# Banded attention of a two-layer decoder: output products moved behind the next group's projections, q, k and v projections in three split terms, head weights streamed in parts

## What is computed

```python
q = einsum('bth,oh->bto', x, wq)      # 16 heads of 128
k = einsum('bth,oh->bto', x, wk)      # 4 heads of 128, each shared by 4 query heads
v = einsum('bth,oh->bto', x, wv)
q, k = rope(q), rope(k)
scores = einsum('btgrd,bsgd->bgrts', q, k) / sqrt(128)
scores = where((s <= t) & (t - s <= 128), scores, min)
out = einsum('bgrts,bsgd->btgrd', softmax(scores), v)
return einsum('bto,ho->bth', out, wo)  # added to x
```

## Time and profile before

| | |
|---|---|
| median of 3 runs | 2412.54 us (2406.25 to 2413.64) |
| the profiled execution | 2406.55 us, span 2404.8 us |
| PE busy over the span | 2151.0 us (89%) |
| DVE busy | 1712.6 us (71%) |
| POOL busy | 1048.7 us (44%) |
| ACT busy | 944.7 us (39%) |
| DMA | 214.87 MB, mean 89 GB/s |

### The profile page before, as it was taken

One profiled execution on the slowest core, in us unless ns is written; L12 is line 12 of the kernel. 1 busy time (PEld: TensorE's weight loads), 2 busy tenths in 40 slices (PEclk: granted clock), 3 DMA queues, 4 the chain that ended last, 5 costly groups with the idle time before them and its releaser, 6 DMA issues. The chain is left out here.

```text
span 2404.8 us, 24923 instructions
## 1 busy us (share of the span) xinstructions
PE 2151.0 (89%) x7344; PEld 1108.7 (46%) x7344; DVE 1712.6 (71%) x2983; ACT 944.7 (39%) x1808; POOL 1048.7 (44%) x798
## 2 busy tenths in 40 slices
PE   6998999899999977997889898999789999999858
PEld 2554445454455543443555555465333433334234
DVE  1787788768876885786889889889546364654554
ACT  1443344333333433764655646465123232332311
POOL 2343354333333440322899998999511011010142
PEclk9999999999999998998999999999889999999979
DMA  7000000000000002455644526353332122221121
GB/s 263 19 19 18 19 20 20 18 18 22 22 18 19 23 23 90 159 186 214 266 162 166 197 105 210 127 203 108 107 80 78 41 77 57 70 70 46 52 109 53
DMA packets 95563, 214.87 MB, mean 89 GB/s; under 512 B 15832, under 2 KB 33112, under 8 KB 93032
## 3 DMA queue, kind: packets, MB, share of 16 engines
q1 hardware_dynamic: 77192, 156.18, 19.8%
q10 hardware_dynamic: 17760, 57.42, 6.7%
...
q0 software_dynamic: 512, 0.13, 0.0%
...
## 5 line engine op out<-in xcount | busy, mean ns | idle before, releaser
L759 POOL TENSOR_SCALAR a_prob<-a_prob,a_rsum 128x256 f32<-128x256 f32 x256 | 146.6, 590 | 467.3 <-DVE a_rsum L687 467.1
L1455 POOL TENSOR_TENSOR s_state<-s_b_rows,s_delta_u 128x1024 f32<-128x1024 f32 x128 | 303.5, 2384 | 36.9 <-DMA s_b_rows<-scan_bc 34.4
L1499 DVE TENSOR_TENSOR_SCAN s_state<-s_decay,s_state 128x512 f32<-128x512 f32 x256 | 304.9, 1211 | 15.5 <-ACT s_decay L1441 13.2
L1614 PE MATMUL c_bank<-c_xn_parts,c_w_parts 128*128 128x512 f32 (+1 forms) x1056 | 269.5, 405 | 6.2 <-DMA c_w_parts<-ffn_weights_lo 6.2
L1441 ACT ACTIVATE s_decay<-s_delta,s_a 128x512 f32<-128x512 f32 x256 | 173.5, 689 | 226.1 <-DVE s_state L1499 220.6
L491 PE MATMUL a_bank<-a_xn_t,a_wq 128*128 128x512 f32 x512 | 227.3, 592 | 0.0
L602 ACT ACTIVATE a_prob<-a_score,a_neg_m 128x256 f32<-128x256 f32 x256 | 117.6, 475 | 279.0 <-DVE a_neg_m L682 278.8
L1614 PEld LDWEIGHTS c_bank<-c_xn_parts,c_w_parts 128*128 128x128 f32 (+1 forms) x1056 | 196.3, 187 | 65.8 <-issue 20.3
L574 PE MATMUL a_bank<-a_wo,a_out_t 128*128 128x512 f32 x512 | 222.3, 593 | 0.0
L2049 ACT ACTIVATE d_prob_t<-d_score 128x512 f32<-128x512 f32 x256 | 138.9, 595 | 192.2 <-PE d_score L1931 191.1
L373 DVE TENSOR_SCALAR f_picks<-f_mask,f_lut_xor,f_lut 128x260 int32<-128x260 int32 x512 | 202.3, 468 | 9.6 <-DVE f_mask L367 0.5
...
...
## 6 DMA issues: line engine op xcount, KB each, us to landing
s_b_rows<-scan_bc SPq DMA_DIRECT2D x64, 512.0 KB, 3.7
c_w_parts<-ffn_weights_hi ACTq DMA_DIRECT2D x39, 512.0 KB, 3.6
c_w_parts<-ffn_weights_lo ACTq DMA_DIRECT2D x39, 512.0 KB, 4.5
...
d_qs<-d_hi SPq DMA_DIRECT2D x128, 64.0 KB, 2.0
d_ks<-d_hi SPq DMA_DIRECT2D x128, 64.0 KB, 2.0
d_factor<-in_factors SPq DMA_DIRECT2D x16, 512.0 KB, 3.6
```

Of the source, the lines that this page charges most:

```text
L1455: pool.tensor_tensor(self.state[:, s], row.broadcast_to([P, 2, T]), self.delta_u[:, h % 2], ALU.mult) \
L1499: dve.tensor_tensor_scan(self.state[:, s, e, :], self.decay[u % 2][:], self.state[:, s, e, :], 0.0, ALU.mult, ALU.add).then_inc(self.scann ...
L1614: mm = nc.tensor.matmul(banks[b][0:width[o], :], w_parts[:, n % SLOTS, w, at:at + width[o]], xn_parts[:, x_, k, :], start=((k, w, x_) == t ...
```

## The change

Three things change in the attention stage.

First, the weights of the projections and the normalized features are kept as two f32r parts, a rounded one and the remainder, and a bank of q, k or v is the sum of three products (both rounded parts, and each remainder with the other's rounded part): 12 single instructions for 8. The features are drained by both engines, ACT rounding and DVE subtracting. Head weights no longer stay in SBUF. SP loads each head's raw weights (256 KB), ACT rounds and POOL subtracts, SP stores both parts in DRAM, and later passes load them from there, 512 KB a head, each when the head's bank of the group before is full. `passes` writes the first pass out apart from the loop.

Second, PE computes the output products of group g - 1 in group g, behind its projections and ahead of its turns. In group 0 the values of the same batch row stand there. Group 3 has its own output products at its end too.

Third, the groups take 4, 4, 3 and 5 chunks of the lookup instead of 4 each. DVE's adds stand between the picks and choices of the chunks, the loads of wo and of the batch rows of x are issued by SP and not by ACT, and the second and third rope of a group follow the exponentials of both later heads.

```diff
+    GROUPS = (0, 4, 8, 11, PER_PASS)
...
+class HeadWeights:
...
+    def load_piece(self, sp, m, source):
+        if m >= 2:
+            sp.wait_ge(self.split, m - 1)
+        sp.dma_start(self.raw[:, m % 2, :], source).then_inc(self.raw_in[m % 2], 16)
+    def load_raw(self, sp, n, p):
+        if n:
+            sp.wait_ge(self.stored[p], 16 * n)
+        self.load_piece(sp, self.piece(n, p), self.dram["head_w"][:, n * self.STEPS + p, :])
+    def load_parts(self, sp, g, p, after_stores=None):
+        if after_stores:
+            sp.wait_ge(self.stored[p], 16 * after_stores)
+        sp.dma_start(self.parts[:, p].bitcast(F32), self.scratch["head_parts"][:, g * self.STEPS + p]) \
+            .then_inc(self.ready[p], 16)
+    def store(self, sp, n):
+        for p in range(self.STEPS):
+            sp.wait_ge(self.ready[p], 16 * (n + 1))
+            sp.dma_start(self.scratch["head_parts"][:, n * self.STEPS + p], self.parts[:, p].bitcast(F32)) \
+                .then_inc(self.stored[p], 16)
+    def round_piece(self, act, m, hi):
+        act.wait_ge(self.raw_in[m % 2], 16 * (m // 2 + 1))
+        self.nc.scalar.copy(hi, self.raw[:, m % 2, :]).then_inc(self.rounded, 1)
+    def round(self, act, n, steps):
+        for p in steps:
+            self.round_piece(act, self.piece(n, p), self.parts[:, p, 0, :])
+    def subtract(self, pool, n, steps):
+        for p in steps:
+            m = self.piece(n, p)
+            pool.wait_ge(self.rounded, m + 1)
+            self.nc.gpsimd.tensor_tensor(self.parts[:, p, 1, :], self.raw[:, m % 2, :],
+                                         self.parts[:, p, 0, :].bitcast(F32), ALU.subtract) \
+                .then_inc(self.ready[p], 16)
...
+            if g < LAST:
+                order += proj(g + 1) + (wo_steps(g - 1) if g else v_steps)
             elif more:
-                order += xn_steps + proj(0)
+                order += xn_steps + wo_steps(g - 1) + proj(0)
+            else:
+                order += wo_steps(g - 1)
             order += [("turn", g, 0, 0), ("turn", g, 1, 0), ("turn", g, 1, 1), ("pv", g, 0),
                       ("turn", g, 2, 0), ("turn", g, 2, 1), ("pv", g, 1),
                       ("turn", g, 3, 0), ("turn", g, 3, 1), ("pv", g, 2), ("pv", g, 3)]
-            order += [("wo", g, tt) for tt in range(TT)]
-        return order + (v_steps if more else [])
+        return order + wo_steps(LAST)
...
+    TERMS = ((0, 0), (1, 0), (0, 1))
...
+            for p in range(heads.STEPS):
+                heads.load_raw(sp, 0, p)
             sp.dma_start(cos2[:], dram["cos2"]).then_inc(w_in["rope"], 16)
             sp.dma_start(sin2[:], dram["sin2"]).then_inc(w_in["rope"], 16)
-            load_queries(sp, 0)
-            sp.dma_start(wv[:], dram["wv_t"].rearrange("(k p) o -> p k o", p=P)).then_inc(w_in["wv"], 16)
             lookup.load_table(sp)
-            with sp.Fori(0, B) as i:
-                lookup.sync(sp, i)
+            heads.store(sp, 0)
+            for p, step in enumerate(proj(0)):
+                consumed(first, 0, step)
+                heads.load_raw(sp, 1, p)
+            load_values(0)
+            sp.dma_start(wo[:], dram["wo_t"].rearrange("(h p) o -> p h o", p=P)).then_inc(w_in["wo"], 16)
+            for b in range(1, B):
+                sp.dma_start(x[:, b], dram["x"][b].rearrange("(t p) d -> p t d", p=P)).then_inc(x_in, 16)
+            def one_pass(i, more):
+                first_pass, last_pass = (isinstance(i, int) and i == at for at in (0, B - 1))
+                for g in range(KV):
+                    chunks = lookup.chunks(g)
+                    ahead = 3 if g == LAST else 1
+                    lookup.sync(sp, i, chunks[:ahead])
+                    if first_pass and g == 0:
+                        for k in range(1, KD):
+                            load_values(k)
+                    if first_pass and g < LAST:
+                        heads.store(sp, g + 1)
+                    if not last_pass or g + 2 < KV:
+                        for p, step in enumerate(proj((g + 1) % KV)):
+                            consumed(ring, i, step)
+                            if first_pass and g < LAST and p == REPS:
+                                lookup.sync(sp, i, chunks[1:2])
+                            if first_pass and g + 2 < KV:
+                                heads.load_raw(sp, g + 2, p)
+                            else:
+                                heads.load_parts(sp, (g + 2) % KV, p,
+                                                 after_stores=KV if first_pass and g + 2 == KV else None)
+                    lookup.sync(sp, i, chunks[2 if first_pass and g < LAST else ahead:])
+                lookup.store(sp, i, lookup.PER_PASS - 1)
...
+            def in_terms(bank, weights_of, xn_of):
+                for n, (wp, xp) in enumerate(TERMS):
+                    for k in range(KD):
+                        mm = nc.tensor.matmul(bank, weights_of(wp, k), xn_of(xp, k),
+                                              start=(n == 0 and k == 0),
+                                              stop=(n == len(TERMS) - 1 and k == KD - 1))
+                return mm
+            def project(ring, in_pass, i, g, steps):
                 for step in steps:
-                    w = wk[:, :, g * HD:(g + 1) * HD] if step[0] == "k" else \
-                        wq[:, :, (g * REPS + step[2]) * HD:(g * REPS + step[2] + 1) * HD]
-                    b, turn = ring.at(step, i)
+                    p = proj(g).index(step)
+                    pe.wait_ge(heads.ready[p], 16 * (i * KV + g + 1))
+                    b, turn = ring.at(step, in_pass)
                     pe.wait_ge(ring.free[b], turn)
-                    for k in range(KD):
-                        mm = nc.tensor.matmul(banks[b][:], w[:, k, :], xn_t[:, k, :],
-                                              start=(k == 0), stop=(k == KD - 1))
-                    mm.then_inc(ring.full[b], 1)
+                    in_terms(banks[b][:], lambda part, k: heads.parts[:, p, part, k * HD:(k + 1) * HD],
+                             lambda part, k: xn_t[:, part, k, :]).then_inc(ring.full[b], 1)
...
             def one_pass(i, more):
-                for g in range(KV):
-                    if g == KV - 1 and more:
-                        norm_tensor(nc, pe, norm, consts.ident, ring, banks, i + 1, in_pass=i)
-                    ng = (g + 1) % KV
-                    nxt = proj(ng) if more or ng else []
+                for g in range(LAST):
                     scores(i, g, (0, 1))
-                    if ng == 0 and more:
-                        ring.wait_free(pe, i, consumed=xn_steps)
-                    project(ring, i, ng, nxt[0:2])
-                    scores(i, g, (2,))
-                    project(ring, i, ng, nxt[2:3])
-                    scores(i, g, (3,))
-                    project(ring, i, ng, nxt[3:])
-                    pe.wait_ge(prob_ready, i * HEADS + (g + 1) * REPS)
-                    turn_probs(i, g, 0, 0)
-                    turn_probs(i, g, 1, 0)
-                    turn_probs(i, g, 1, 1)
-                    for tt in range(TT):
-                        weigh(i, g, tt)
-                        if tt + 2 < TT:
-                            turn_probs(i, g, tt + 2, 0)
-                            turn_probs(i, g, tt + 2, 1)
-                    pe.wait_ge(w_in["wo"], 16)
-                    for tt in range(TT):
-                        ring.wait_free(pe, i, ("wo", g, tt), consumed=[("pv", g, tt)])
-                        b, _ = ring.at(("wo", g, tt), i)
-                        for r in range(REPS):
-                            mm = nc.tensor.matmul(banks[b][:], out_t[:, tt, r * P:(r + 1) * P],
-                                                  wo[:, g * REPS + r, :],
-                                                  start=(r == 0), stop=(r == REPS - 1))
-                        mm.then_inc(ring.full[b], 1)
+                    project(ring, i, i, g + 1, proj(g + 1)[0:2])
+                    scores(i, g, (2, 3))
+                    project(ring, i, i, g + 1, proj(g + 1)[2:])
+                    if g:
+                        outputs(i, g - 1)
+                    else:
+                        values(i)
+                    weighted(i, g)
+                scores(i, LAST, (0, 1))
                 if more:
-                    values(ring, i)
+                    norm_tensor(nc, pe, norm, consts.ident, ring, banks, i + 1, in_pass=i)
+                    outputs(i, LAST - 1)
+                    scores(i, LAST, (2, 3))
+                    ring.wait_free(pe, i, consumed=xn_steps)
+                    project(ring, i, i + 1, 0, proj(0))
+                else:
+                    scores(i, LAST, (2, 3))
+                    outputs(i, LAST - 1)
+                weighted(i, LAST)
+                outputs(i, LAST)
...
+                    lookup.pick(i, chunks[1])
+                    take_output(i, g, 0)
```

(8 more changed lines are left out.)

337 lines of the change are left out of this document (230 added, 107 removed).

## The result

The changed kernel takes **2463.3 us** (median of 4 runs, 2459.5 to 2468.6), the one before 2411.0 (4 runs): ratio **1.0218**, 95% interval 1.0198 to 1.0238. It is slower, as the likeliest case said, but by 52 us where 6 were forecast, and outside the range.

A forecast was written before the change was run, and what follows sets the result against it. It took PE and DVE as both nearly full, with DVE late. Start +0.2, casts +1.5, three passes -8.4 and last pass +14.8 summed to +8.1 us; with a base of 2409.5 it forecast 2418 us, range 2382 to 2442.

The forecast's parts named there:

- Split terms: Projections on PE: 12 instructions a bank at 2.9 us instead of 8 at 3.5, 61 us of PE work less.
- the walk of DVE: Middle group timed step by step from its first maximum; DVE's own path takes 48 to 50.3 us, just beneath the group's 51.6.
- Middle groups: Groups 0 to 2: DVE's third add at +39.5 gates PE's third turn, half clock follows; 50.9, 51.6 and 51.9 us.
- rival by late chunks: Second index chunk at +26 rather than +24 in every group, nine groups 2 us longer: 2436 us, chance 0.24.
- Group 3: Last group of the earlier passes: third turn waits for a rope that DVE reaches at +40.9; 66.2 us long.
- Last group: End of the last pass: inverses behind four adds and two chunks' picks; 54.2 us, against 41.9 before.
- +14.8: Loss in us of the last pass, forecast at 208.3 against 193.5 before.
- Start and first pass: Stage's start and first-pass casts: late first index chunk and ACT's casts ahead of swaps, priced at +0.2 and +1.5 us.
- +0.2: Start: first index chunk lands near 67 us behind wo and x, judged by an 8 KB table's 9.7 us; start 63.3 against 63.12.
- +1.5: ACT's casts ahead of the swaps in groups 0 and 1, 1.2 us each, partly absorbed by the chunk wait; loss in us.
- start "not held up": Rival: first index chunk isn't delayed by the loads of wo and x, 22 us less, 2396 us; chance 0.15.
- third add in time: Rival: bank free near +34.5, no slow clock, DVE's path sets groups of 46.7, 47.9 and 46; 2352 us, chance 0.12.

The follow-up runs named there:

- e5: Changed kernel with all five of group 3's ropes ahead of the third chunk's picks on DVE; 2446.8 us, ratio 1.0147 to the kernel before.
- e6: Changed kernel with the last group's inverses of heads 3 and 4 behind the first chunk's picks; 2457.8 us, ratio 1.0192 to the kernel before.
- e1: Changed kernel with only the first index chunk put ahead of wo and x on SP's queue; 2460.0 us, ratio 1.0206 to the kernel before.
- e3: e1 with the loads of wo and x spread over groups 0 to 2 of the first pass; 2448.7 us, ratio 1.0148 to the kernel before.
- e13: e9 with POOL's rope sum of the second query ahead of the fourth head's scaling; 2385.8 us, ratio 0.9892 to the kernel before.
- e14: e13 with the first pass's casts and subtractions behind swaps and rope sums, SP's loads in that order; 2382.2 us, ratio 0.9882 to the kernel before.
- e4: Changed kernel with all four of DVE's output adds ahead of the third chunk's picks in groups 0 to 2; 2429.7 us, ratio 1.0075.
- e12: e13 with the second index chunk loaded at the group's start and its picks ahead of DVE's last rope; 2372.6 us, ratio 0.9847.
- e9: Changed kernel with the edits of e3, e4, e5 and e6 together; 2389.3 us, ratio 0.9916 to the kernel before.

## Why the prediction was right, and where it failed

**Split terms: right.** 60 instructions in 14.34 us are 2.87 a bank (forecast 2.8 to 2.9), and this was worth nearly nothing, as the walk of DVE said.

**Middle groups: right in time, half right in cause.** The third add was forecast at +39.5 and came at +39.7, half clock behind it, groups 51.5 to 53.4 for 51 to 52; PE's wait was 1.5 and 3.6 us rather than one of 4 to 6. But DVE doesn't wait for the second index chunk (SP issues it at 384.74, +20.4; the picks wait for a rope instead). The walk left out that ACT's swap must wait for POOL's rope sums, which have two buffers: its sentence "ACT's swap, two copies of 0.58, and DVE's last rope (0.7) end at +21.7" is the one that failed, the rope ended at +24.9. The wait on POOL took just the place of the wait on the chunk, forecast to end at +24; that they agree within 1 us is luck. POOL's sums end at 392.63 now, beside the masks and before the picks (2.69 us); both together take 6.5 us, forecast 6.7. The rival by late chunks didn't occur either, for the same reason.

**Group 3: the mechanism right, a term too small.** The third turn came at +44.7 for +40.9, 3.8 late; from there to the end the turns to the outputs took 10.98 us (513.88 to 524.86) for 8.4 and 0.9. Together these are 5.5 of the 6.4 us missed in this pass; over three passes group 3 missed 4.8, 6.4 and 4.9. In the walk DVE "reaches" the rope; in the trace DVE, POOL and ACT wait for each other in turn. e5 takes that chain off the picks and gives about 6 us a group back.

**Last group: right.** 53.9 for 54.2, and the reason (inverses behind adds and picks) is confirmed by e6. The "+14.8" sets a pass counted to the end of its last add against one counted to its start; like for like the last pass lost 17.0 (210.5 against 193.5).

**Start and first pass: this is the step that failed**, with 22 of the 45.6 us (27.2 less the 4.8 of group 3). "+0.2" for the start and "+1.5" for ACT's casts were both mis-sized. The chunk landed at 73.3 and not near 67 (6.3 us: SP reached wo at 50.2, not 46, and its issues of x held it until 61.28). Behind the chunk group 0 took 57.9 us instead of 47.3 (10.6), group 1 57.8 instead of 51.6 (6.2), group 2 0.6 more; less the 1.5 allowed.

Two things that the sum had at nothing stand behind this. The first is a wait: a cast was priced by its length, 0.6 us, but the one of wv stood 19.29 us in ACT's order ahead of the first swaps, because its raw piece was behind the load of wo and x. So e1, which brings only the chunk forward, shortens group 0 by 3.6 us, and e3, which spreads the load, by 17. The second is POOL. The prediction counts its subtractions up to the start, and none in the groups. In group 0 POOL takes 18.0 us from its product for the first query's rope to the sum that the last swap waits for (80.96 to 98.98), with four subtractions in it, and 12.3 in the second pass (323.37 to 335.71) without them; in group 1 two subtractions put DVE's last rope 3.3 us later. Later ones slow DVE's lookup beside them, in group 1 by 1.7 us. ACT's casts of head weights were not what counted here: they waited 1.7 and 0.7 us in group 0 and not at all in group 1, each time ahead of swaps that POOL held up longer. In e3 and e13, where a part of wo goes ahead of the raw loads, the casts do wait, 6.5 and 6.2 us in group 0. e14, which moves casts and subtractions together, gives 4.9 us back, so what each is worth was read from the traces and not shown by a run of its own.

**The rivals.** The start "not held up" was priced at 22 us; with the queue cleared it gave 17, so as a mechanism it was real, and as a forecast of the change it was wrong, as the prediction argued from the 8 KB table. The third add in time was priced at 58 us; e4 gives 34, because the same walk that puts DVE's path "just beneath" at 48 to 50.3 left out 5.2 us of waiting in it. e12 fills that wait, on top of e9's edits, and its groups of 47.2, 48.2 and 49.5 us come near the 46.7, 47.9 and 46 of that rival.
